# Attention pooling on one Trainium2 core: a third chunk in plain fp32, and the softmax's division moved into the copy of each pooled pair

## The reference

```python
W_b, W_c = (fc1_w[:E], fc1_w[E:])
h = relu(einsum('bse,eh->bsh', behavior_emb, W_b) + (candidate_emb @ W_c)[:, None, :] + fc1_b)
scores = einsum('bsh,h->bs', h, fc2_w[:, 0]) + fc2_b[0]
attn = softmax(scores, axis=-1)
user_interest = einsum('bse,bs->be', behavior_emb, attn)
x = concatenate([user_interest, candidate_emb], axis=1)
z = relu(x @ mlp1_w + mlp1_b)
logit = (z @ mlp2_w + mlp2_b)[:, 0]
```

## Time and profile before

| | |
|---|---|
| median of 3 runs | 267.96 us (267.91 to 269.76) |
| the profiled execution | 267.95 us, of which the span is 266.1 us |
| TensorE busy, mean granted clock | 254.9 us (96%), 0.993 |
| VectorE, ScalarE, GpSimd busy | 205.4, 198.6, 28.9 us |
| transfers | 105.80 MB, mean 398 GB/s |

### The profile page before, as it was taken

How to read it: one execution, slowest core, us unless ns; L and a number is a source line. 1 busy time by engine, 2 the same in 40 slices (tenths; PEclk the granted TensorE clock), 3 DMA queues, 4 the chain that set the end, 5 groups by cost and what they waited for, 6 DMA issues and landing times.

```text
span 266.1 us, 10392 instructions
## 1 busy us (share of the span) xinstructions
PE 254.9 (96%) x3944; PEld 215.3 (81%) x3944; DVE 205.4 (77%) x316; ACT 198.6 (75%) x482; POOL 28.9 (11%) x39
## 2 busy tenths in 40 slices
PE   8989798979999999999999999999999999999795
PEld 7547587868888888888888888888888888888664
DVE  0458976977889796979798896979798997969221
ACT  2469685985969698896969696997887997957111
POOL 2000201102020110202020110202020201102100
PEclk9999799999999999999999999999999999999999
DMA  7999999999999999999999999999999999999700
GB/s 246 427 429 426 426 423 420 423 420 426 426 427 431 425 425 421 429 429 425 431 427 423 425 425 429 427 429 423 423 429 425 429 427 427 427 421 424 320 2 0
DMA packets 10684, 105.80 MB, mean 398 GB/s; under 512 B 1200, under 2 KB 1712, under 8 KB 2864
## 3 DMA queue, kind: packets, MB, share of 16 engines
q1 hardware_dynamic: 10384, 105.44, 94.3%
q10 hardware_dynamic: 288, 0.20, 0.2%
HBM read 105.63 MB, written 0.00 MB: 397 GB/s over the span
## 4 chain that ended last, share of the span: by engine, by line
PE 88%; DMA 4%; issue 3%; DVE 2%; SPq 1%; ACT 1%; DVEq 0%; ACTq 0%
PE z_ps L665 18%; PE s_ps L682 17%; PE z_ps L666 16%; PE z_ps L669 16%; PE u_ps L694 16%; DMA xt<-in_behavior_t 4%; PE z_ps L694 1%; PE z_ps L733 1%; PE z_ps L776 1%; SPq L263 1%; PE z_ps L770 1%; ACT hidden_rest L411 0%; DVE xl L500 0%; PE z_ps L757 0%; SPq L267 0%
## 5 line engine op out<-in xcount | busy, mean ns | idle before, releaser
L500 DVE TENSOR_TENSOR xl<-xt,xh 128x800 fp32r<-128x800 f32 x120 | 117.0, 1005 | 2.9 <-ACT xh L369 2.7
L369 ACT CAST xh<-xt 128x800 fp32r<-128x800 f32 x120 | 98.4, 888 | 10.7 <-DMA xt<-in_behavior_t 10.7
L665 PE MATMUL z_ps<-xh,w_hi 128*128 128x512 f32 x240 | 85.5, 356 | 2.4 <-ACT hidden_rest L411 1.2
L411 ACT ACTIVATE hidden_rest<-z_ps,bias 128x200 f32<-128x200 f32 x192 | 66.3, 428 | 28.0 <-PE z_ps L669 24.9
L666 PE MATMUL z_ps<-xh,w_lo 128*128 128x512 f32 x240 | 80.4, 349 | 0.0
L669 PE MATMUL z_ps<-xl,w_hi 128*128 128x512 f32 x240 | 64.2, 349 | 0.4 <-DVE xl L500 0.4
L665 PEld LDWEIGHTS z_ps<-xh,w_hi 128*128 128x128 f32 x240 | 45.5, 189 | 16.6 <-issue 4.4
L510 DVE TENSOR_TENSOR hidden_rest<-z_ps,neg_bias 128x800 f32<-128x800 f32 x48 | 47.2, 984 | 5.4 <-PE z_ps L669 3.0
L340 POOL TENSOR_TENSOR weights_by_row<-weights,masks_sb 128x400 f32<-128x400 f32 x31 | 27.0, 870 | 222.3 <-DVE xl L500 177.6
L666 PEld LDWEIGHTS z_ps<-xh,w_lo 128*128 128x128 f32 x240 | 45.5, 190 | 5.7
L694 PE MATMUL u_ps<-x,weights_by_row 128*32 128x128 f32 (+1 forms) x1680 | 44.8, 262 | 4.0 <-issue 4.0
(11 more groups left out here) (70 smaller groups left out, 94.0 us busy)
## 6 DMA issues: line engine op xcount, KB each, us to landing
x<-in_behavior SPq DMA_DIRECT2D x31, 1600.0 KB, 20.4
xt<-in_behavior_t SPq DMA_DIRECT2D x30, 1600.0 KB, 18.2
xt<-in_behavior_t SPq DMA_DIRECT2D x4, 400.0 KB, 4.9
xt<-in_behavior_t SPq DMA_DIRECT2D x2, 800.0 KB, 7.7
x<-in_behavior SPq DMA_DIRECT2D x1, 832.0 KB, 13.3
x<-in_behavior SPq DMA_DIRECT2D x1, 768.0 KB, 14.7
later_sb<-in_later SPq DMA_DIRECT2D x1, 258.5 KB, 23.4
first_sb<-in_cand_rest SPq DMA_DIRECT2D x1, 192.0 KB, 5.7
```

The source lines that it names most:

```text
L369: nc.scalar.copy(xh_of(q, g)[:, :], xt[q][:, g, :]).then_inc(xh_made, 1)
L411: op = nc.scalar.activation(hidden_of(q, g)[:, :, mine], z[:, :, mine], ACT.Relu, bias=bias[:, bass.ds(c * ROWS + g * EACH + b, 1)])
L500: nc.vector.tensor_tensor(xl[g][:, :], xt[q][:, g, :], xh_of(q, g)[:, :].bitcast(F32), ALU.subtract).then_inc(xl_made, 1)
L665: nc.tensor.matmul(z[:, a:b], w_hi[:, :], xh_of(q, g)[:, a:b], start=True, stop=False)
```

## The change

Two things. First, `WHOLE` goes from 2 to 3: chunk 2 is multiplied in plain fp32 from `xt` too, so its four casts and four subtractions are gone, and the waits that count high and low halves shift by a chunk. Second, the division by the sum of weights moves. `weight_sums` has two columns, one for each chunk of a pair. Between the two weighted sums of a pair TensorE does the new `row_sums`: eight column-tiled matmuls of one column each, with masks of 32 columns (`pair_rows`) as weights, into a free column of the scores' bank. It waits until the exponents are made and until VectorE has taken the scores out of that bank. VectorE takes one reciprocal of 128x1 after the seven softmax steps, and `copy_pooled4` on ScalarE scales by it in place of a plain copy, with one wait more. `exponents` waits for the row sums of the pair before. At the end, `spread_inverses`, `normalise`, the spreading by a mask and two masks are gone; `mlp_pooled(0)` comes before the row sums of the last pair, and `logits(0)` comes before the last chunk's weighted sum. The masks' load shrinks from 228 to 84 columns.

```diff
--- before.py
+++ after.py
@@ -32,13 +32,13 @@
...
 PHASE_AT = 1
-WHOLE = 2
+WHOLE = 3
 WARM_UP = 9
...
 FIRST_COLS = {"w_c": P, "cand_t": 4 * P}
-MASK_COLS = {"row_mask": 3 * ROWS, "fold": Q, "row_first": ROWS, "own_row": EACH, "same_row": P}
+MASK_COLS = {"row_mask": 3 * ROWS, "fold": Q, "own_row": EACH}
 LATER_COLS = {"w_mlp": 4 * P, "b_mlp": 2, "w_out": 2, "b_out": 1}
...
@@ -94,7 +94,7 @@
...
         weights_by_row = [sb(f"weights_by_row{i}", [P, TILES, 2 * ROWS]) for i in range(2)]
-        weight_sums = sb("weight_sums", [P, CHUNKS])
+        weight_sums = sb("weight_sums", [P, 2])
...
@@ -112,11 +112,13 @@
...
         w_c, cand_t = (part_of(first_sb, FIRST_COLS, n) for n in FIRST_COLS)
-        row_mask, fold, row_first, own_row, same_row = (part_of(masks_sb, MASK_COLS, n) for n in MASK_COLS)
+        row_mask, fold, own_row = (part_of(masks_sb, MASK_COLS, n) for n in MASK_COLS)
         w_mlp, b_mlp, w_out, b_out = (part_of(later_sb, LATER_COLS, n) for n in LATER_COLS)
...
         pair_half = [slice(0, ROWS), slice(ROWS, 2 * ROWS)]
+        pair_rows = [row_mask[:, ROWS:], row_mask[:, 0:2 * ROWS]]
         row_mask = row_mask[:, ROWS:2 * ROWS]
...
@@ -147,9 +147,9 @@
...
         last_pair_ps = end_banks[0][0]
-        inverse_ps = [end_banks[0][1], end_banks[2][0]]
         mlp_ps = [end_banks[1], [s_ps[:, :], u_ps[:, :]]]
-        logit_ps = [end_banks[2][1], inverse_ps[0]]
+        logit_ps = [end_banks[2][1], end_banks[0][1]]
+        row_sums_ps = s_ps[:, 2 * RUN * Q:2 * RUN * Q + 1]
...
@@ -373,13 +372,17 @@
...
                     act.wait_ge(masked, c - 1)
+                    act.wait_ge(row_sums_done, c - buf)
                 nc.scalar.activation(weights[buf][:, :].rearrange("p (r t) -> p r t", t=RUN), score_runs(buf), ACT.Exp,
                                      bias=exp_bias[buf][:, :],
-                                     accum_out=weight_sums[:, bass.ds(c, 1)]).then_inc(weights_made, 1)
+                                     accum_out=weight_sums[:, buf:buf + 1]).then_inc(weights_made, 1)
             def copy_pooled4(c, bank):
+                act.wait_ge(inv_made, c + 1)
                 act.wait_ge(pooled_done, c + 1)
-                nc.scalar.copy(pooled4[:, :], bank[:, 0:P]).then_inc(pooled4_copied, 2)
+                nc.scalar.mul(pooled4[:, :], bank[:, 0:P], inv_sums[:, :]).then_inc(pooled4_copied, 2)
...
@@ -423,7 +426,7 @@
...
                     arrived = (xt_loaded[nq], loads(c + 1, nq)) if g == 0 else None
-                    high_half(c + 1, nq, g, arrived, phase < (WHOLE if g < 2 else 2 * WHOLE - 1))
+                    high_half(c + 1, nq, g, arrived, phase < (WHOLE if g < 2 else WHOLE + 1))
...
@@ -436,6 +439,10 @@
...
                     return
+                if phase == 1:
+                    biased_relu(c, q, 1, phase)
+                    biased_relu(c, q, 3, phase)
+                    return
                 if q % 2 == 1:
...
@@ -443,7 +450,8 @@
...
                     return
-                high_half(c, q, 3, None, phase == WHOLE)
+                if phase >= WHOLE:
+                    high_half(c, q, 3, None, False)
                 biased_relu(c, q, 1, phase)
...
@@ -455,7 +463,7 @@
...
             periods(period, (CHUNKS - FIRST) // X_BUFS - 1)(act)
-            copy_pooled_t(LAST - 4, u_ps[:, P:P + 2 * ROWS])
+            copy_pooled_t(LAST - 4, last_pair_ps[:, P:P + 2 * ROWS])
             for n in range(2):
...
@@ -541,26 +549,12 @@
...
-            def inverses(part, step):
-                a, b = PART_CHUNKS[part]
-                row_sums = inverse_ps[part]
-                if step == 1:
-                    dve.wait_ge(row_sums_done, part + 1)
-                    op = nc.vector.reciprocal(inv_sums[:, a:b], row_sums[:, 0:b - a])
-                if step == 2:
-                    dve.wait_ge(mlp_step[part], 1)
-                    op = nc.vector.tensor_tensor(
-                        inv_sel[:, a:b, :], inv_sums[:, a:b].unsqueeze(2).to_broadcast([P, b - a, ROWS]),
-                        row_first.unsqueeze(1).to_broadcast([P, b - a, ROWS]), ALU.mult)
-                op.then_inc(mlp_step[part], 1)
-            def normalise(part):
-                a, b = PART_CHUNKS[part]
-                inv = inverse_ps[part]
-                dve.wait_ge(inv_done, part + 1)
-                dve.wait_ge(pooled_t_copied, b + 2)
-                nc.vector.tensor_tensor(pooled_n[:, a * ROWS:b * ROWS], inv[:, 0:(b - a) * ROWS],
-                                        pooled_t[:, (a + 2) * ROWS:(b + 2) * ROWS], ALU.mult).then_inc(mlp_step[part], 1)
+            def inverses(c):
+                dve.wait_ge(row_sums_done, c + 2)
+                dve.wait_ge(pooled4_copied, c + 2)
+                nc.vector.reciprocal(inv_sums[:, :], row_sums_ps).then_inc(inv_made, 2)
...
@@ -585,20 +579,25 @@
...
                     return
+                if phase == 1:
+                    biased_max(c, q, 2, phase)
+                    return
                 if q % 2 == 1:
-                    if phase > 1:
-                        low_half(c, q, 3)
+                    low_half(c, q, 3)
                     next_low(0)
...
                     return
-                low_half(c, q, 2)
-                low_half(c, q, 3)
+                if phase >= WHOLE:
+                    low_half(c, q, 2)
+                    low_half(c, q, 3)
                 if phase == 2:
...
                     softmax(c - 2, n, phase == 2)
+                if phase > 2:
+                    inverses(c - X_BUFS)
                 next_low(0)
...
@@ -621,14 +620,11 @@
...
-            inverses(0, 1)
-            inverses(0, 2)
             for n in range(PAIR_STEPS):
                 softmax(LAST - 1, n, False)
+            inverses(LAST - 3)
             mask_last()
-            normalise(0)
-            inverses(1, 1)
-            inverses(1, 2)
+            inverses(LAST - 1)
...
@@ -654,7 +649,8 @@
...
-                    arrivals = [[*xt_piece, xt_loaded[0]], [xt_half, xt_half, xt_loaded[1], xt_loaded[1]]][c]
+                    arrivals = [[*xt_piece, xt_loaded[0]], [xt_half, xt_half, xt_loaded[1], xt_loaded[1]],
+                                GROUPS * [xt_loaded[2]]][c]
                     pe.wait_ge(arrivals[g], 16)
...
@@ -669,12 +665,9 @@
...
-            def score(c, q, taken):
+            def score(c, q):
                 pe.wait_ge(hidden_made, c * HALF + HALF)
                 pe.wait_ge(relu_made, c * HALF + HALF)
-                if taken is not None:
-                    pe.wait_ge(softmax_step, taken)
...
@@ -743,20 +736,17 @@
...
-            def row_sums(part):
-                a, b = PART_CHUNKS[part]
-                pe.wait_ge(weights_made, b)
-                pe.wait_ge(relu_made, LAST * HALF + part + 1)
-                nc.tensor.matmul(inverse_ps[part][:, 0:b - a], same_row, weight_sums[:, a:b],
-                                 start=True, stop=True).then_inc(row_sums_done, 1)
-            def spread_inverses(part):
-                a, b = PART_CHUNKS[part]
-                pe.wait_ge(mlp_step[part], 2)
-                nc.tensor.matmul(inverse_ps[part][:, 0:(b - a) * ROWS], ones[:, :],
-                                 inv_sel[:, a:b, :].rearrange("p c r -> p (c r)"),
-                                 start=True, stop=True).then_inc(inv_done, 1)
+            def row_sums(c, scores_of):
+                pe.wait_ge(weights_made, c + 2)
+                pe.wait_ge(softmax_step, pair_steps(scores_of) + 2)
+                for n in range(2):
+                    for g in range(GROUPS):
+                        op = nc.tensor.matmul(row_sums_ps[g * Q:(g + 1) * Q, :], pair_rows[n],
+                                              weight_sums[:, n:n + 1], start=n == 0, stop=n == 1,
+                                              tile_position=(0, g * Q))
+                op.then_inc(row_sums_done, 2)
...
@@ -764,7 +754,8 @@
...
                 if part == 1 and m == 0:
-                    pe.wait_ge(softmax_step, pair_steps(LAST - 1) + 2)
+                    pe.wait_ge(inv_made, CHUNKS)
                 if part == 1 and m == 1:
...
@@ -772,9 +763,9 @@
...
                 a, b = (n * ROWS for n in PART_CHUNKS[part])
-                pe.wait_ge(mlp_step[part], 3)
-                nc.tensor.matmul(mlp_ps[part][m][:, 0:b - a], w_mlp[:, 0, m * P:(m + 1) * P], pooled_n[:, a:b],
-                                 start=False, stop=True).then_inc(z_all_done, 1)
+                pe.wait_ge(pooled_t_copied, PART_CHUNKS[part][1] + 2)
+                nc.tensor.matmul(mlp_ps[part][m][:, 0:b - a], w_mlp[:, 0, m * P:(m + 1) * P],
+                                 pooled_t[:, 2 * ROWS + a:2 * ROWS + b], start=False, stop=True).then_inc(z_all_done, 1)
...
@@ -807,7 +798,7 @@
...
                         bias_products(1)
-                    if phase == 1 and g == 3:
+                    if phase == WHOLE - 1 and g == 3:
                         pe.wait_ge(w_lo_made, 1)
...
@@ -819,38 +810,43 @@
...
```

(45 more changed lines are left out.)

## The result

The changed kernel takes 267.07 us (median of 8 runs, 266.66 to 267.24) against 267.94 us before (8 runs): ratio 0.9963, 95% interval 0.9949 to 0.9977. That is 0.9 us faster, inside the range and nearer to no change than the 266.2 forecast. The profiled execution is one of the quicker ones, 266.79 us with a span of 265.0; its sums are made against 267.95 and 266.1.

The account below looks back on a forecast made before the run. TensorE's chain was taken to bound the kernel from 59 us on, with transfers close behind. From 267.95 us, -0.3 up to the loop's end and -1.4 in the end part gave 266.2 us; range 264.7 to 270.2.

Parts of the forecast that it names:

- The start of chunk 2 and the clock: Early chunks: plain chunk 2 gains 1.0 us, the clock staying at 2.4 GHz 1.4; second pair's scores near 34.8.
- The row sums: Between a pair's weighted sums in the loop: 0.15 us a pair, +2.1 us over 14 pairs, ends 1.5 and 4.1.
- An issue floor of 25 ns: Rival, chance 0.15: the row sums' tiny matmuls start 25 ns apart, 0.40 us a pair, total 270.2 us.
- VectorE's reciprocal and the scaled copy: In the loop: the reciprocal's delay is hidden from TensorE, and ScalarE's scaled copy costs what the plain one did.
- -2.4 + 2.1 = -0.3 up to the loop's end: Up to the loop's end: 2.4 us won at the start, 2.1 lost to row sums, 0.3 us gained.
- the floor of -0.55 isn't reached: At chunk 31's second group: loads let at most 0.55 us of earlier gains through; the -0.3 stays short of that.
- a pair takes over 15.0 us: In the loop: a sign that the prediction is wrong; it expected 14.9 us a pair.
- -1.4 for the end part: End part: last weighted sum starts 1.1 us earlier and `normalise` goes for 0.3; ends -1.0 and -1.8.
- The standstills: Rival, chance 0.15: TensorE's "issue" pieces of 1.0 to 1.5 us, perhaps waits for code, shift with the changed code length.
- one may vanish: End part: one TensorE "issue" piece may disappear, giving 264.7 us; part of a rival with chance 0.15.
- the sum of -1.7: Whole kernel: 0.3 us gained up to the loop's end and 1.4 in the end part, from 267.95 to 266.2 us.

Follow-up runs that it names:

- the filler: Kernel before, with five unused matmuls with ones put where TensorE waits for VectorE at 28.7 to 29.8 us: 267.64 us, ratio 1.0003.
- the third chunk alone: Kernel before with only the third chunk in plain fp32 and no row sums: 267.65 us, ratio 0.9996.
- half the loads: Changed kernel loading only 13 of 25 tiles of each untransposed chunk, weighted sums rereading those (pooled values not the reference's): 264.05 us, ratio 0.9871.
- an execution 1.2 us late at 69 us: Profiled execution of the changed kernel with the first part's logits moved back behind the last chunk's weighted sum: 266.55 us, ratio 0.9951.
- the division alone: Changed kernel with `WHOLE = 2`, so only two chunks in plain fp32: 267.55 us, ratio 1.0001.
- the tripled row sums: Changed kernel with every row sum done three times over, 32 more instructions a pair: 277.42 us, ratio 1.0368.
- the end part's further version: Changed kernel, end part reordered, chunk 28's row sums ahead of the last scores, candidates' second matmul and first logits behind the last weighted sum: 265.63 us, ratio 0.9924.
- the plain reordering: Changed kernel, end part reordered: first part's MLP ahead of weighted sum 28, transpose behind weighted sum 30, logits behind weighted sum 31: 265.40 us, ratio 0.9902.
- ScalarE's relu first: Changed kernel with ScalarE's relu of group 3 ahead of exponents and copy in the even chunks' periods: 278.31 us, ratio 1.0384.

## Why the prediction was right or wrong

**The start of chunk 2 and the clock: right.** 34.80 for the second pair's scores, where 34.8 was forecast, and a clock of 1.00 from 29 to 34, behind idle of 1.17 us where 1.1 was forecast. That the fall answered to the idle is shown by the filler. The figure owes something to luck: the first scores of the same code start between 20.2 and 21.3 in the profiles here.

**The row sums: right.** 0.14 us a pair against 0.15, by the two kernels that differ in them (14.83 and 14.69). An issue floor of 25 ns is refuted: 15 start within 0.12 us, and even added ones cost 12 ns. VectorE's reciprocal and the scaled copy stayed hidden.

**-2.4 + 2.1 = -0.3 up to the loop's end: a good number, in part by luck.** At the place for which the prediction worked out its floor, the second group of chunk 31, the lead is 0.26 us (241.05 against 241.31). But the way there was another. The step that failed is "the floor of -0.55 isn't reached", with the floor set at that one place and by VectorE alone. The ceiling of the loads acts from 187 us on: the lead was still 1.44 there, more than the 2.4 less ten row sums at 0.15, because the pairs before took 14.76 us up to that point and the new ones 14.83, only 0.07 more, and the loads then took 1.04 of it in three pairs. Those take 15.15 to 15.28 us, the prediction's own sign of being wrong ("a pair takes over 15.0 us"). At the second group of chunk 31 VectorE's max has ended 0.47 us before TensorE needs it (240.58); it is ScalarE's relu, one group later, that holds TensorE, and by the fourth group of chunk 31 (243.48 against 243.50) nothing of the lead is left. Three runs show the ceiling: the third chunk alone wins 1.5 us at the start and nothing in time, half the loads give 1.1 us at the last scores, and an execution 1.2 us late at 69 us is on time at 232.

**-1.4 for the end part: mis-sized.** It was 1.11: 0.39 between the start of that fourth group and the last scores (1.33 in place of 1.72), where the old row sums stood, and 0.72 behind. `logits(0)` cost 0.49, as charged (0.45), and the step of `normalise` gave back 0.34. What went wrong is `spread_inverses(0)` at 0.86: some 0.2 us of that is the change from column-tiled to full matmuls, which went to the next in line (the candidates' matmuls take 1.70, before 1.50). The new row sums of the last pair stand between full matmuls, so they and the transpose behind them cost 0.24 + 0.34, where I had charged 0.15 and nothing for the transpose's 0.19. And ScalarE's scaled copy doesn't cost what the plain one did: in the end part, where TensorE waits for it, it takes 0.37 us against 0.27. Since -0.3 came out as next to nothing and -1.4 as -1.11, the sum of -1.7 was 1.13 us by the starts.

**The standstills: the rival was named and underpriced.** They didn't move much (1.36 against 1.53 at the end, 2.76 against 2.49 in the loop's first turn), so the forecast didn't suffer; that they stayed is luck, as the same part with two plain chunks had none at the end. But the largest gain in reach was there, and I had "one may vanish" as chance, not as something an order of steps decides.

**The rest** is the choice of execution: the profile's is 1.16 us quicker than the one before, the medians differ by 0.87.

## What to carry to other kernels

When an engine's chain runs from end to end and the transfers are full as well, compare the two rates per period (14.8 and 15.3 us here): the slower one collects at the end whatever the faster one wins earlier, and by itself only work behind the last landing is worth taking away. A lead that is worth nothing alone can still pay for work that is added before that point. Instructions that are run for the first time can have a price of their own under full transfers, which code in a loop pays once; put matmuls with many columns, and so few instructions, where a new stretch of code begins. Before moving a step of an engine with slack, look at which other engines its end sets off, and what they will then run beside.

## What the runs showed of the hardware

A wait for code under full transfers took 0.76 (the division alone) to 2.27 us (the tripled row sums). The one in the end part vanished when the transfers were over, when 3.2 us of slow instructions came first, and when TensorE came there 1.8 us later (the division alone). The Trainium skill (Runtime: NRT & Kernel Launch, instruction fetch mechanics) has blocks of 16 KB, as the packets here, and a cost of crossing from one to the next that is mostly hidden. These standstills don't agree, if they are waits for code as argued above: ahead of the last one TensorE did 130 matmuls and as many weight loads in 4.3 us, some 60 instructions a us.

Idle in such waits was followed by a granted clock of 1.2 GHz after 1.88 us in the end part's further version, and after 1.59 and 2.27 us with the tripled row sums (1.67 us there was not). It was not after 1.88 us in the plain reordering, nor after 1.95 us with the division alone. So the length of the idle alone doesn't decide it; what does is open.

Column-tiled matmuls of one column start 7 to 8 ns apart when 16 stand between weighted sums (15 in 0.12 us), and 32 more cost 12 ns each (0.38 us a pair). The Trainium skill (TensorE: Matmul & The Clock Gate, back-to-back issue gap) gives a floor of about 25 ns for any small matmul; none of these runs shows it for four tiles side by side.

A 128x800 subtract on VectorE took 1.6 us beside a 128x400 multiply on POOL (3.24 for two, ScalarE's relu first), 0.97 alone.
